# Three fp32r products for the first phase's projections, one activation table, joined scans: an RWKV, mixture-of-experts and attention kernel

## The reference

```python
shifted = jnp.pad(x, ((0, 0), (1, 0), (0, 0)))[:, :-1]
xk = x * time_mix_k + shifted * (1.0 - time_mix_k)      # likewise xv, xr
k = jnp.einsum('btc,dc->btd', xk, Wk)                   # likewise v, r
def step(carry, kv):                                    # over the tokens
    num, den, mx = carry
    max_out = jnp.maximum(mx, kt + u)
    e1 = jnp.exp(mx - max_out); e2 = jnp.exp(kt + u - max_out)
    out = (e1 * num + e2 * vt) / (e1 * den + e2)
    max_st = jnp.maximum(mx + w, kt)
    e1s = jnp.exp(mx + w - max_st); e2s = jnp.exp(kt - max_st)
    return (e1s * num + e2s * vt, e1s * den + e2s, max_st), out
x = _layernorm(x + (sigmoid(r) * wkv) @ Wo.T)
# then: the 2 best of 8 experts of each token, softmax of their two logits as weights
```

## Time and profile before

| | |
|---|---|
| median of three runs | 407.81 us |
| the profiled execution, its own time | 410.51 us |
| its span, first to last instruction | 408.6 us |
| busy share of the span | PE 92%, PEld 80%, DVE 72%, ACT 51%, POOL 32% |
| first phase (until the first turned tile of the second) | 0 to 117 us |
| second phase | 117 to about 232 us |
| third phase | from about 232 us |
| mean granted TensorE clock | 0.973 |

### The profile page before, as it was taken

The page is one execution under the profiler, slowest core; times in us unless marked ns, Lnnn a source line. Parts: engine busy times, 40 slices in busy tenths (PEclk is TensorE's granted clock), DMA queues, the critical chain, the costliest instruction groups (busy, mean ns, idle before and its releaser), DMA issues.

```text
span 408.6 us, 7333 instructions
## 1 busy us (share of the span) xinstructions
PE 373.9 (92%) x2234; PEld 325.4 (80%) x2234; DVE 293.4 (72%) x774; ACT 208.7 (51%) x435; POOL 129.6 (32%) x226
## 2 busy tenths in 40 slices
PE   8999999999858999999999858999999999999781
PEld 8888888888747776777777656898999899999680
DVE  4978999999975455797453265686969687886642
ACT  5474577557745333455335322556555645645451
POOL 2002355544645500002301077435344340401111
PEclk9999999999979999999999987999999999999987
DMA  7842864301133456533431132102020200000000
GB/s 219 279 173 86 121 219 136 104 33 53 52 90 118 134 178 199 163 107 100 131 116 52 53 91 65 53 1 77 2 79 2 77 29 2 26 2 26 2 26 26
DMA packets 28565, 35.75 MB, mean 87 GB/s; under 512 B 3696, under 2 KB 25712, under 8 KB 28272
## 3 DMA queue, kind: packets, MB, share of 16 engines
q1 hardware_dynamic: 19696, 21.78, 18.0%
q0 software_dynamic: 3072, 8.39, 6.3%
q10 hardware_dynamic: 5760, 5.12, 3.6%
HBM read 22.83 MB, written 12.45 MB: 86 GB/s over the span
## 4 chain that ended last, share of the span: by engine, by line
PE 47%; DVE 28%; ACT 8%; issue 7%; POOL 7%; DMA 1%; SPq 0%; ACTq 0%; POOLq 0%; DVEq 0%
PE bank L400 18%; PE bank L547 10%; PE bank L568 8%; DVE st L1047 4%; POOL arena L1638 3%; POOL nm L1575 2%; PE bank L527 2%; PE bank L557 2%; PE bank L736 2%; DVE arena L1107 2%; PE bank L410 2%; DVE arena L1110 2%; POOL rs L1572 2%; DVE arena L1481 2%; ACT arena L798 1%
## 5 line engine op out<-in xcount | busy, mean ns | idle before, releaser
L400 PE MATMUL bank<-arena 128*128 128x256 f32 (+2 forms) x576 | 116.6, 357 | 1.7 <-issue 0.7
L400 PEld LDWEIGHTS bank<-arena 128*128 128x128 f32 x576 | 99.8, 190 | 14.8 <-DVE arena L1463 2.0
L798 ACT ACTIVATE arena<-bank 128x256 f32<-128x256 f32 (+1 forms) x118 | 45.5, 422 | 45.7 <-PE bank L568 30.1
L547 PE MATMUL bank<-gu,arena 128*128 x156 | 53.9, 469 | 0.0
L1570 POOL TENSOR_TENSOR ve<-mv,eps 128x2 f32<-128x2 f32 x32 | 6.8, 213 | 145.4 <-DVE mv L1051 143.6
L803 ACT ACTIVATE arena<-arena,nm,rs 128x256 f32<-128x256 f32 x48 | 26.2, 596 | 38.5 <-POOL nm L1575 38.4
L568 PE MATMUL bank<-dn,arena 96*128 x156 | 41.1, 386 | 4.6 <-DVE arena L1261 3.8
L1638 POOL DMA_INDIRECT arena<-yg,ypos x32 | 31.3, 977 | 38.9 <-DMA yg<-arena 30.5
L1261 DVE COPY arena<-bank 96x256 f32<-96x256 f32 x39 | 16.3, 419 | 36.1 <-PE bank L557 32.6
L568 PEld LDWEIGHTS bank<-dn,arena 96*128 96x128 f32 x156 | 28.6, 190 | 14.8 <-issue 6.9
L1610 POOL DMA_INDIRECT xg<-x,pos x32 | 34.3, 1073 | 14.6 <-issue 7.3
(11 more groups left out here) (211 smaller groups left out, 864.1 us busy)
## 6 DMA issues: line engine op xcount, KB each, us to landing
arena<-xg SPq DMA_DIRECT2D x39, 128.0 KB, 2.0
yg<-arena ACTq DMA_DIRECT2D x39, 128.0 KB
arena<-in_xT SPq DMA_DIRECT2D x8, 256.0 KB
x<-in_x SPq DMA_DIRECT2D x8, 256.0 KB, 4.7
out<-arena SPq DMA_DIRECT2D x8, 256.0 KB
gu<-in_w_gate SPq DMA_DIRECT2D x1, 1408.0 KB, 7.8
gu<-in_w_up SPq DMA_DIRECT2D x1, 1408.0 KB, 7.2
dn<-in_w_down SPq DMA_DIRECT2D x11, 128.0 KB, 5.2
```

The source lines that it names most:

```text
L400: last = pe.matmul(dst, l, r, start=i == 0, stop=i == len(pairs) - 1)
L547: last = pe.matmul(bank[BANK_GU[i % 2]][:, 0:2 * F], xtT[:, i % 2, chunk(k)], w[:, :, k, :, bass.ds(e, 1), :], start=k == 0, stop=k == KC - 1)
L798: return act.activation(dst, src, ACT.Copy)
```

## The change

- The projections' fp32 products become three fp32r products each: weights and inputs are split into a rounded part (hi) and the rest (lo), and hi*hi + hi*lo + lo*hi is summed. A slot has 72 fp32r products in place of 24 fp32 ones.
- The split costs new work. Before the slots: twelve ACT copies of 128x256 (`weights_high`), twelve DVE operations (`weights_low`), each waiting for ACT's. Per sequence: one ACT copy of 128x512 (`xs_high`) and one DVE subtraction of 128x512 (`xs_low`) that waits for it. In slot s, ACT does `xs_high(s + 2)` behind `keys(s + 1)`, and DVE does `xs_low(s + 2)` between `finish_y` and `states(s)`.
- Sigmoid is folded in: the gate is exp(-r) (a Relu that bounds it, then Exp), and (1 + exp(-r)) multiplies the denominator ahead of its logarithm. The two table loads of a slot are gone, and d_ok comes at the end of `outputs`.
- The six scans of 256 in a slot become three of 512, with a row of decay values (wfull) and a reset column.
- The casts sel and pos leave DVE's slot: sel is one copy in `token_slots`, pos moves to POOL's `scatter`. The routing weights come from an exponential on ACT and three POOL operations, except for the last two sequences.
- dn's clearing and the two pick rows move on DVE from the very start to behind the weights and `xs_low(1)`. The load of the Silu table moves from ahead of `silu(0)` to ahead of `turned(1)`.
- SP's load of xT waits for `xs_low` in place of r.

The core of the diff:

```diff
+        wA_hi = [mixing(kv_hi, "a b"), mixing(fh, "a b c"), mixing(w1q, "a b")]
+        wA_lo = [mixing(kv_lo, "a b"), mixing(fl, "a b c"), mixing(w3q, "a b")]
...
                 if j == 0:
-                    pe.wait_ge(in_xsb[b % 2], 16 * (b // 2 + 1))
+                    pe.wait_ge(xsl_ok, b + 1)
                 if b == 0:
-                    pe.wait_ge(cleared, 1)
-                    pe.wait_ge(wcur_ok, j + 1)
-                    pe.wait_ge(wprev_ok, j + 1)
-                s = xs[b % 2]
+                    pe.wait_ge(wlow_ok, j + 1)
                 for d in range(KC):
                     last = product(dst[:, d, :], [
-                        (wA[:, j, lag * KC + k, chunk(d)], s[:, k, 1 - lag:1 - lag + T])
-                        for k in range(KC) for lag in range(2)])
+                        pair for k in range(KC) for lag in range(2)
+                        for pair in split([w[j][:, lag * KC + k, chunk(d)] for w in (wA_hi, wA_lo)],
+                                          [s[b % 2][:, k, 1 - lag:1 - lag + T] for s in (xs_hi, xs_lo)])])
                 last.then_inc(done, 1)
...
+            def weights_high(j):
                 act.wait_ge(in_kvr[j], 16)
                 for k in range(KC):
-                    last = act.activation(wA[:, j, k, :], raw_kvr[:, j, k, :], ACT.Copy,
-                                          scale=vec[:, k, MIX + j:MIX + j + 1])
-                last.then_inc(wcur_ok, 1)
+                    act.activation(wA_hi[j][:, k, :], raw_kvr[:, j, k, :], ACT.Copy,
+                                   scale=vec[:, k, MIX + j:MIX + j + 1])
+                    last = act.activation(wA_hi[j][:, KC + k, :], raw_kvr[:, j, k, :], ACT.Copy,
+                                          scale=unmix[:, k, j:j + 1])
+                last.then_inc(whigh_ok, 1)
+
+            def xs_high(b):
+                act.wait_ge(in_xsb[b % 2], 16 * (b // 2 + 1))
+                past(act, rp_mm, b - 1)
+                copy(xs_hi[b % 2][:, :, 1:], xs[b % 2][:, :, 1:]).then_inc(xsh_ok, 1)
+
+            steps = [0]
+
+            def stepped(op):
+                op.then_inc(act_step, 1)
+                steps[0] += 1
+                act.wait_ge(act_step, steps[0])
+
+            weights_high(0)
+            xs_high(0)
+            weights_high(1)
+            weights_high(2)
...
             def keys(b):
                 act.wait_ge(kp_mm, b + 1)
                 past(act, carg_ok, b)
                 if b == 0:
                     act.wait_ge(cleared, 1)
-                copy(kS[:, :, 1:], halves(0)).then_inc(k_ok, 1)
+                copy(kS[:, :, 1:], halves(0))
                 for k in range(KC):
...
                 act.wait_ge(rp_mm, s + 1)
-                past(act, z_ok, s)
-                act.activation(gate[:, :, :], halves(3), ACT.Tanh, scale=0.5).then_inc(gate_ok, 1)
+                past(act, d_ok, s)
+                stepped(act.activation(gate[:, :, :], halves(3), ACT.Relu, bias=floor[:, :]))
+                act.activation(gate[:, :, :], gate[:, :, :], ACT.Exp, bias=floor[:, :], scale=-1.0).then_inc(gate_ok, 1)
...
                 keys(new)
+                if s + 2 < B:
+                    xs_high(s + 2)
                 if 0 <= old:
-                    gaps(old)
+                    odds(old)
...
                 if 0 <= s:
-                    act.preload_act_table_set("natural_log_exp_and_others")
                     reciprocal(s)
...
             copy_x1T(B - 3)
             exponentials(B - 1)
-            gaps(B - 3)
-            act.preload_act_table_set("natural_log_exp_and_others")
+            odds(B - 3)
             turned(0)
             reciprocal(B - 1)
+            act.preload_act_table_set("silu_and_others")
             turned(1)
             normalise_x1(B - 2)
             turned(2)
             copy_x1T(B - 2)
-            act.preload_act_table_set("silu_and_others")
             silu(0)
...
+            def weights_low(j):
                 dve.wait_ge(in_kvr[j], 16)
+                dve.wait_ge(whigh_ok, j + 1)
                 for k in range(KC):
-                    last = dve.tensor_scalar(wA[:, j, KC + k, :], raw_kvr[:, j, k, :], unmix[:, k, j:j + 1], None,
-                                             ALU.mult)
-                last.then_inc(wprev_ok, 1)
+                    dve.scalar_tensor_tensor(wA_lo[j][:, k, :], raw_kvr[:, j, k, :], vec[:, k, MIX + j:MIX + j + 1],
+                                             wA_hi[j][:, k, :].bitcast(F32), ALU.mult, ALU.subtract)
+                    last = dve.scalar_tensor_tensor(wA_lo[j][:, KC + k, :], raw_kvr[:, j, k, :], unmix[:, k, j:j + 1],
+                                                    wA_hi[j][:, KC + k, :].bitcast(F32), ALU.mult, ALU.subtract)
+                last.then_inc(wlow_ok, 1)
+
+            def xs_low(b):
+                dve.wait_ge(xsh_ok, b + 1)
+                dve.tensor_tensor(xs_lo[b % 2][:, :, 1:], xs[b % 2][:, :, 1:], xs_hi[b % 2][:, :, 1:].bitcast(F32),
+                                  ALU.subtract).then_inc(xsl_ok, 1)
+
+            weights_low(0)
+            xs_low(0)
+            weights_low(1)
+            weights_low(2)
             dve.wait_ge(wdec_ok, 1)
+            for k in range(KC):
+                last = dve.tensor_copy(wfull[:, k, :], wdec[:, k:k + 1].broadcast_to([P, T]))
+            last.then_inc(wdec_ok, 1)
+            dve.wait_ge(wdec_ok, 2)
+            dve.memset(wfull[:, 1, 0:1], LOW).then_inc(wdec_ok, 1)
+            xs_low(1)
+            dve.memset(dn[0:FE, 1, :, :], 0.0).then_inc(cleared, 1)
+            dve.wait_ge(pick_ok, 1)
+            dve.memset(pick[0:1, :].bitcast(F32), 1.0)
+            dve.memset(pick[64:65, :].bitcast(F32), 1.0).then_inc(rows_ok, 1)
+            dve.wait_ge(wdec_ok, 3)
...
+                dve.tensor_tensor_scan(row(mM, 0, KC * T), row(wfull, 0, KC * T), row(kP, 0, KC * T), LOW, ALU.add,
+                                       ALU.max).then_inc(wkv_step, 1)
...
-                dve.tensor_tensor(dd[:, :, :], den[:, :, :], eC[:, :, :], ALU.add).then_inc(d_ok, 1)
+                dve.tensor_tensor(dd[:, :, :], den[:, :, :], eC[:, :, :], ALU.add).then_inc(wkv_step, 1)
                 dve.wait_ge(cv_ok, s + 1)
-                dve.tensor_tensor(nn[:, :, :], num[:, :, :], nn[:, :, :], ALU.add).then_inc(wkv_step, 1)
+                dve.tensor_tensor(nn[:, :, :], num[:, :, :], nn[:, :, :], ALU.add).then_inc(z_ok, 1)
                 dve.wait_ge(wkv_step, 4 * s + 4)
                 dve.wait_ge(gate_ok, s + 1)
-                dve.scalar_tensor_tensor(nn[:, :, :], gate[:, :, :], 1.0, nn[:, :, :], ALU.add,
-                                         ALU.mult).then_inc(z_ok, 1)
+                dve.scalar_tensor_tensor(dd[:, :, :], gate[:, :, :], 1.0, dd[:, :, :], ALU.add,
+                                         ALU.mult).then_inc(d_ok, 1)
...
                     finish_y(now)
+                if s + 2 < B:
+                    xs_low(s + 2)
                 states(s)
...
+                pool.tensor_scalar(topw[:, tiles_of(b), 1], gap[:, :], 1.0, None, ALU.add).then_inc(topw_ok, 1)
+                pool.wait_ge(topw_ok, 3 * b + 1)
+                pool.tensor_tensor(topw[:, tiles_of(b), 0], topw[:, tiles_of(b), 1], negone[:, :], ALU.pow).then_inc(topw_ok, 1)
+                pool.wait_ge(topw_ok, 3 * b + 2)
+                pool.tensor_tensor(topw[:, tiles_of(b), 1], topw[:, tiles_of(b), 0], gap[:, :], ALU.mult).then_inc(topw_ok, 1)
 
             def scatter(b):
+                pool.wait_ge(route_step, 4 * b + 4)
+                pool.tensor_copy(pos[:, tiles_of(b), :], pos_f[:, tiles_of(b), :]).then_inc(pos_ok, 1)
```

More of the change, by code:

```diff
@@ L46 @@
 FULL_AT = 5
+GATED = B - 2
+SIGMOID_FLOOR = 40.0
 FIRST = -(-(2 * FULL_AT * T - E * (P - 1)) // P)
@@ L204, in then @@
             return at(place[0], shape)
-        wA = at(0, (3, 2 * KC, C))
-        xs = [then(KC, 1 + T) for _ in range(2)]
+        wfull = at(0, (KC, T))
+        xs = [at(3 * 2 * KC * C, (KC, 1 + T)), then(KC, 1 + T)]
         wo1 = then(KC, C)
@@ L494, in a_slot @@
                 if 0 <= new < B:
-                    past(pe, k_ok, new)
                     past(pe, ku_ok, new)
@@ L521, in turn @@
                 if i == 0:
-                    pe.wait_ge(k_ok, B)
                     pe.wait_ge(ku_ok, B)
@@ L844, in exponentials, with odds @@
                 act.wait_ge(rp_mm, s + 1)
-                past(act, z_ok, s)
-                act.activation(gate[:, :, :], halves(3), ACT.Tanh, scale=0.5).then_inc(gate_ok, 1)
+                past(act, d_ok, s)
+                stepped(act.activation(gate[:, :, :], halves(3), ACT.Relu, bias=floor[:, :]))
+                act.activation(gate[:, :, :], gate[:, :, :], ACT.Exp, bias=floor[:, :], scale=-1.0).then_inc(gate_ok, 1)
+            def odds(b):
+                act.wait_ge(route_step, 4 * b + 1)
+                past(act, topw_ok, 3 * b)
+                for t in range(NT):
```

(41 more changed lines are left out.)

119 lines of the change are left out of this document (62 added, 57 removed).

## The result

| | before | changed |
|---|---|---|
| median of the runs | 407.8 us | 436.7 us (436.01 to 437.25, 4 runs) |
| ratio | | 1.0707, 95% interval 1.0689 to 1.0726 |
| profiled execution: own time, span | 410.5, 408.6 us | 436.0, 434.3 us |
| mean granted clock of PE | 0.973 | 0.927 |
| a slot in the steady part | 13.70 us | 17.05 us |

The kernel is slower by 7.1%. The prediction was 431.5 us, with a range of 426 to 440. The time lies in the first phase: between the two profiled executions 26.4 us are lost until the eighth `exponents` starts, and from there to the end 0.7 us are won.

The account below looks back on a forecast made before the run. PE and DVE together were taken to bound the slot. Start and slots summed to +23.3 us, +22.4 after slots 6 and 7, +23.7 with the passage: 407.8 + 23.7 = 431.5 us, range 426 to 440.

Parts of the forecast that it names:

- The wait in the slot: In slots 0 to 5, DVE at xs_low stands still for ACT's xs_high: 3.4 us, bounds 2.8 and 4.2.
- The slots: First phase: slots of 17.1 us, +3.4 each, from +3.4 wait, -0.6 dropped work and +0.6 xs_low.
- The joined scans: On DVE in a slot: three joined scans save 0.06 us each, between 0 and 0.1.
- rival (a): Slots and start: the wait plus PE's clock falling, up to +12, 443 us; costly form, over 440, chance 0.10.
- The start: Before slot 0: weight copies and splits delay PE's first product to 7.7; exponents(0) starts at 15.4, not 9.97: +5.4 us.
- The clearing of dn: At the start on DVE: 1.76 us, formerly hidden, now adds to the path to exponents(0).
- The GpSimd worry: POOL's weight operations delay the norm, with ACT behind, by up to 0.3 us; counted as nothing, 0.3 x 5 in upper end.
- the pair of rows: POOL's norm pair takes 1.45 us beside DVE's work and 0.50 at 127.77, agreeing with contended SBUF interfaces.
- The passage: From first to second phase: later d_ok and the moved Silu load cost +1.3 us, bounds 0.5 and 2.5.
- The rule on table loads: In the passage: the skill's 2.66 us per table switch with drain would cost 1.4 more than the trace's 1.28.
- From the profile to the median: Whole kernel: median taken 2.7 us under the profiled execution, so profiled 434.2 and median 431.5 us.
- the mild form of (a): Part of the upper bound of 440: PE's clock falls as in rival (a), short of its costly form; no own size.

Follow-up runs that it names:

- the second profile of before: The kernel before, unchanged, profiled once more: ratio 1.0011, profiled execution 407.55 us.
- The two experiments at the start: Changed kernel with dn's clearing, pick rows and table load moved earlier: 435.1 us; changed kernel with 24 warm-up products, not 9: 436.8 us.
- the second pair: Change without fp32r products, Silu load ahead: 411.2 us; the same with Silu load back, dn's clearing and table load ahead at the start: 408.8 us.

## Why the prediction held, step by step

- **The wait in the slot: right.** Predicted 3.4 us of standing still (4.0 in slot 0), ACT needing 5.1 us from L1091's end (L1150 now). Measured 3.34 in the steady slots, 3.96 in slot 0, and 5.13 us from L1150's end to the end of `xs_high`. The two unknown operations, taken as 0.7 and 0.6, were 0.70 and 0.63 from start to start. What the prediction had right is the method: not the engines' busy sums, which say that there is room, but the two lists laid beside each other in order of time, from the last event that both share.
- **The slots:** predicted 17.1, measured 17.05. Slot 0 took 4.4 us more (predicted 4.4), slot 1 0.7 more (0.9), slots 2 and 3 6.6 (5.8), slots 4 and 5 6.7 (6.8), slot 6 0.7 less (0.6 less; it took 13.49, which fits the sum's 13.6 and not the 13.1 that the prediction names among its signs). The miss is slot 2, where DVE stood still for 4.33 us and not 3.4. The prediction had seen that slots 2 and 3 of before were 1.04 us too long, put it down to ACT's Ln behind a table load, and struck it out with the load. The load went, but 1 us stayed. ACT gets the norm late there:

```profile
49.76 1.09 ACT L808 ACTIVATE x<-x,nm,rs 128x256 f32<-128x256 f32 x2 [8.37 <-POOL nm L1637]
...
52.61 0.62 ACT L862 ACTIVATE arena<-arena 128x510 f32<-128x510 f32 x1
```

ACT starts the norm 0.85 us after the slot's start (48.91), in the steady slot 0.09 after it (84.07), and the exponentials at 52.61, 1.04 us after L1150's end (51.57) and not 0.08. POOL's pair L1637 took 1.93 us ahead of it in place of 1.52, and slot 1 is 0.3 us shorter behind DVE's statistics, having no `positions` yet. In before the same lateness stood there (the norm at 35.92, 0.77 after 35.15). So the condition "ACT starts right after L1091" failed in this one slot, and ACT's own list set the wait.
- **The joined scans** were to give 0.06 each; the first is 1.23 in place of 1.27, the others 1.22 and 1.19.
- **PE:** products 0.119 us apart at the full clock, as taken from the third phase. Its busy time in a slot was to be 11.8; it is 14.1 in the changed kernel, at a mean clock of 0.90, and 12.4 at a clock of 1.00 in the kernel with `xs_low` last. Nothing hangs on it. The clock fell in the slots, as rival (a) had it, and cost nothing there, since PE had 3 us to spare.
- **The start: the step that was mis-sized.** Predicted +5.4 us, measured +8.65 (+7.65 against the second profile of before). Three things were left out. ACT's first weights copy started at 4.67, not 3.62, because the table load now stands right behind the wait for vec's DMA and ahead of the copies (1.05 us; with the load moved back it started at 3.89). The first k ran at half clock after a stop of PE of 3.2 us; I had named this price, 2.9 at most, and put it into the rival and not into the sum (1.55). And DVE took 0.36 us more to issue the clearing of dn; some 0.3 are small gaps. The two experiments at the start gave 3.4 and 1.55 us back.
- **The clearing of dn** was priced as it came: 1.76 us, in the open.
- **The GpSimd worry did not bite in the steady slots.** In slot 2 POOL's pair was part of the 1 us above, by its length and not by the weight operations. The three weight operations took 0.24, 0.73 and 0.20 us and ended at 97.41, DVE's statistics at 98.42. The norm waited for DVE and not the other way round. What the pair of rows stood for is real, though, and came out at full size where a long POOL operation was put beside DVE.
- **The passage:** +1.3 predicted. The Silu load's share is 1.4, by the pair of kernels that differ in it alone, and 1.3 by the second pair. As a whole the passage can't be read to better than some 3 us, because two executions of before differ by that. In the changed kernel PE is at half clock through most of it:

```profile
137.00:149.00 12.00, 9.24 (x24) 5.89 (x24) 9.07 (x26) 5.11 (x10) 6.74 (x11) 0.50 0.33 101
```

- **The rule on table loads:** the Silu load takes 1.28 us in every profile, and the next operation starts 0.01 to 0.02 us behind it (125.57 above). Nothing of a drain of the same size is to be seen; the trace's price was the right one.
- **From the profile to the median:** the profiled execution of before lay 2.7 us above its median; that of the changed kernel lay 0.7 below its own. I assumed the same offset. Against the profiled execution the forecast, 434.2, was 1.8 us short of 436.0: 3.25 at the start and 0.8 in slots 2 and 3 too little, about 1 in the passage and 0.7 behind it too much; the rest is in small differences. The other 3.4 of the 5.2 us that separate 431.5 from 436.7 are the offset, and the earlier trace rows could not show it, since they come from that one execution with its slow passage. Against the second profile of before, which lay at its median, the passage to tile 4 took 3.1 us more (38.6 against 35.4), where the whole passage was to cost 1.3. How much of that is the change and how much one execution isn't shown: the profiles of the other kernels with the Silu load ahead have 36.9 to 41.2 in the same stretch.
- **The range.** Its bounds for the wait, 2.8 and 4.2 us, don't follow from the numbers beside them: with both unknown operations at 0.5 the wait is 3.0, with both at 0.9 it is 3.8. By these the upper end would be 431.5 + 2.4 + 1.5 + 1.2 = 436.6 before the mild form of (a) is added, and the measured 436.7 lies at that edge. So the number was in the range in part by bounds that were too wide: the start and slot 2 went the same way, and the load that moved and ACT's lateness had no term in the range.

**Where the gain went.** A slot of before was held by two engines at once, PE with 13.70 and DVE with 13.25 us and its latencies. The change takes PE's busy time from 13.70 to 12.44 us and pays for it with 0.6 on DVE, which even without any wait leaves the slot where it was. Placed as it is, the payment also ties DVE to ACT's end, which costs 3.35 us more in each slot.

## What to carry to other kernels

Before a product is split into cheaper ones, count which engine makes the parts, and where in its list that stands: in these lists an operation that waits for another engine held all that was queued behind it, so it belongs where its input has long been there, and one operation moved was worth over 5% here. If two engines are nearly full, relieving one brought nothing here, whatever its busy time said. And price a start by its own list of events, with the clock that PE gets after a stop and the loads that stand behind a wait.

## What the runs showed of the hardware that I had not expected

- **A short DVE operation waits for the whole of POOL's:** 1.30 and 1.10 us in place of 0.20, beside POOL's `tensor_tensor` of 128 x 512 with 1.29 and 1.10 us. DVE's operations with one input in PSUM, or with one input only, lost nothing beside such a POOL operation of 1.29 us.
- **PE's clock falls after it has resumed:** a stop of 3.24 us at the start was followed by 0.6 us of products at the full clock and then by 0.50 for over 3 us. That is one execution: in six other profiles with the same nine warm-up products and a stop of 3.0 to 3.7 us, the very first product is listed at 0.58 us and not 0.39, and the next ones come 0.21 apart. That accounts for some of the difference between starts: with `xs_low` last, keys(0) began at 14.26 in one profile and at 13.41 in the other, `exponents(0)` at 19.36 and 18.51. In the slot from 83.98, with stops of 0.6 and 2.4 us (2.0 and 2.3 in the slot before it), the products of v come 0.119 us apart and those of r, from 98.2 on, 0.21: a part of the slot runs at half clock, for a mean of 0.90.
- **A passage of one kernel differs by 3 us between executions**, and the first `exponents` by 1 us, while the steady slots repeat to 0.03. Slot 1 of the kernel with `xs_low` last took 12.70 us in one profile and 11.87 in the other. For a change of under 1% the profile of the middle says more than one execution's total.
- **The chips differ by 1.3%** for the same kernel (407.9, 410.5 and 413.2 us).
